# Third stage of a four-stage transformer block: who transposes P, and when the value product runs

## The reference

```
ln = layernorm(x)
q = ln @ Wq.T;  k, v = split(ctx @ Wkv.T)          # 16 heads of 32, 128 keys per sequence
s = where(causal, q @ k.T / sqrt(32), lowest)
p = softmax(s)
x = x + tanh(g) * (p @ v) @ Wout.T
```

## Time and profile before

| | |
|---|---|
| median of 3 runs | 1339.49 us (1338.63 to 1339.74) |
| profiled execution | 1338.95 us |
| its span, first to last instruction | 1337.2 us |
| granted TensorE clock | 1.000 |
| busy: TensorE, VectorE, ScalarE, GpSimd | 98%, 70%, 39%, 30% of the span |
| third stage | about 1004 to 1192 us of the span |

### The profile page before, as it was taken

How to read it: one execution, slowest core, us unless ns; L and a number is a source line. 1 busy time by engine, 2 the same in 40 slices (tenths; PEclk the granted TensorE clock), 3 DMA queues, 4 the chain that set the end, 5 groups by cost and what they waited for, 6 DMA issues and landing times.

```text
span 1337.2 us, 20281 instructions
## 1 busy us (share of the span) xinstructions
PE 1314.1 (98%) x7364; PEld 1065.7 (80%) x7364; DVE 937.2 (70%) x1813; ACT 517.5 (39%) x1569; POOL 404.5 (30%) x462
## 2 busy tenths in 40 slices
PE   7999999999999999999999999999998899999998
PEld 6788888888887788778887888788886677778877
DVE  5766676675775878785678667776888788846643
ACT  3545455454564331231123111321126777832220
POOL 3213423231255342201121112113525866630000
PEclk9999999999999999999999999999999999999999
DMA  8755454443572232210221112112324556455651
GB/s 297 229 165 167 151 171 137 157 158 120 190 217 87 88 90 72 83 40 16 57 78 52 31 40 87 44 48 67 99 83 145 198 177 206 163 200 172 218 167 55
DMA packets 137523, 167.92 MB, mean 126 GB/s; under 512 B 16080, under 2 KB 89936, under 8 KB 137424
## 3 DMA queue, kind: packets, MB, share of 16 engines
q1 hardware_dynamic: 137424, 166.63, 39.3%
HBM read 112.05 MB, written 54.53 MB: 125 GB/s over the span
## 4 chain that ended last, share of the span: by engine, by line
PE 88%; DVE 6%; ACT 3%; DMA 1%; issue 1%; POOL 1%; SPq 0%; ACTq 0%; DVEq 0%; POOLq 0%
PE bank L118 86%; PE bank L121 2%; ACT P L124 1%; DVE STG L130 1%; DVE AH L130 1%; DVE XR L140 0%; DVE AH L127 0%; ACT STG L124 0%; SPq L170 0%; DVE st L152 0%; DMA pscr<-STG 0%; DMA XR<-in_x_dram 0%; DMA STG<-in_W1E_dram 0%; DVE sm L146 0%; POOL AR L130 0%
## 5 line engine op out<-in xcount | busy, mean ns | idle before, releaser
L118 PE MATMUL bank<-XT,AR 128*128 128x512 f32 x1152 | 279.7, 392 | 0.1
L118 PE MATMUL bank<-AR 128*128 128x512 f32 x1056 | 257.7, 395 | 1.2 <-DVE AR L130 1.2
L118 PEld LDWEIGHTS bank<-XT,AR 128*128 128x128 f32 x1152 | 214.2, 188 | 47.0 <-ACT STG L124 0.5
L124 ACT ACTIVATE STG<-bank,b1c 128x512 f32<-128x512 f32 x128 | 88.3, 690 | 384.6 <-PE bank L118 318.0
L118 PEld LDWEIGHTS bank<-AR 128*128 128x128 f32 x1056 | 194.5, 188 | 49.1 <-issue 3.7
L118 PE MATMUL bank<-AR,CT 128*128 128x512 f32 x768 | 191.2, 392 | 0.0
L118 PE MATMUL bank<-AR,AH 128*128 128x512 f32 x768 | 185.5, 390 | 0.0
L127 DVE CAST AH<-STG 128x512 fp32r<-128x512 f32 x192 | 92.3, 481 | 110.7 <-PE bank L118 98.7
L118 PEld LDWEIGHTS bank<-AR,AH 128*128 128x128 f32 x768 | 143.9, 188 | 29.7
L118 PEld LDWEIGHTS bank<-AR,CT 128*128 128x128 f32 x768 | 140.2, 188 | 26.7
L127 POOL CAST BA<-STG 128x256 fp32r<-128x256 f32 x64 | 30.5, 477 | 394.5 <-PE bank L118 243.4
(11 more groups left out here) (145 smaller groups left out, 1814.3 us busy)
## 6 DMA issues: line engine op xcount, KB each, us to landing
XR<-scr SPq DMA_DIRECT2D x64, 256.0 KB, 3.1
pscr<-PYZ SPq DMA_DIRECT2D x30, 512.0 KB, 2.9
PYZ<-pscr SPq DMA_DIRECT2D x120, 128.0 KB, 3.0
XR<-in_x_dram SPq DMA_DIRECT2D x32, 256.0 KB, 4.2
XR<-lscr SPq DMA_DIRECT2D x128, 64.0 KB, 2.0
scr<-XR SPq DMA_DIRECT2D x32, 256.0 KB, 2.1
pscr<-STG SPq DMA_DIRECT2D x16, 512.0 KB, 2.6
PTV<-pscr SPq DMA_DIRECT2D x64, 128.0 KB, 2.8
```

The costliest lines, as they stand in the source:

```text
L118: return self.e.matmul(o, w, x, start=start, stop=stop, skip_group_check=True) if self.e else Nothing()
L124: return self.e.activation(o, x, func, **kw) if self.e else Nothing()
```

## The change

P of units 7 to 12 (`whole`) is transposed by VectorE in all four heads: two more block transposes into a new tile P3V, and a second store. DRAM holds both halves side by side (`pscr4`), and each of the four loads brings twice the data, into PTV[:, 0:2048]; the value product of these units reads all four heads in that layout (`P3W`). TensorE's transposes and ScalarE's copies go for these units. In steps 10 to 15 (`late_av`) the value product, and v of the next four sequences where it falls in the step, stand last in the step on TensorE, ScalarE and VectorE, and in steps 9 to 14 the loads stand behind SyncE's other loads. In all steps VectorE transposes P ahead of q's copy. The mask seeds are all ScalarE's (no seeded step has u % 4 = 2). In steps 2 and 3 two x transposes move from the one to the other, and one v product takes bank 4. Waits that named the bank of a transposed P name VectorE's transpose instead where that unit is whole. ScalarE's program has its calls moved as TensorE's.

```
+        P3V = sb("P3V", [128, 1024], F32)
...
+        P3W = PTV[:, 0:2048].rearrange("p (j n c) -> p n j c", j=4, n=16)
...
+        pscr4 = [nc.dram_tensor(f"pscr4{k}", [128, 2048], F32, kind="Internal").ap() for k in range(2)]
...
+        def whole(u):
+            return 7 <= u < 13
+
+        def late_av(u):
+            return 9 <= u < 18 and whole(u - 3)
...
         def by_vector(u):
-            return (0,) if u % 4 == 1 else (0, 1)
+            return () if u % 4 != 2 else (0, 1)
...
             def v3(m):
                 for b in range(4):
                     s = slice(128 * b, 128 * b + 128)
-                    k = ps.take(("v3", m, b), ring3.next())
+                    k = ps.take(("v3", m, b), 4 if (m, b) == (1, 0) else ring3.next())
...
             def turn3(u, ring):
-                for b in (2, 3):
+                for b in () if whole(u) else (2, 3):
...
-                        if j < 2:
+                        if whole(u):
+                            ins = pe.matmul(o.rearrange("p (a c) -> p a c", a=4), V3[:, b, 32 * h:32 * h + 32],
+                                            P3W[:, 4 * j + b], True, True)
+                        elif j < 2:
...
@@ the steps of TensorE @@
-                if 3 <= u < 16 and not k_first(u):
+                if 3 <= u < 16 and not k_first(u) and not late_av(u):
                     av3(u - 3, ring3)
-                if u > 4 and g == 2 and not k_first(u):
-                    v3(m)
+                    if g == 2:
+                        v3(m)
                 if 0 < u < 16:
                     k3(u, ring3)
...
+                if u == 3:
+                    ln_turn(2, 1, 0, ring3.next())
+                    ln_turn(2, 1, 1, ring3.next())
...
-                if u < 16 and g:
+                if u < 16 and g and u != 2:
                     for tb in tiles3(u)[g - 1]:
                         ln_turn(*after3(m), tb, ring3.next())
                 if u < 16 and g == 3 and m + 1 < NM:
                     cx_turn(m + 1, ring3)
                 if u < 16 and g == 3:
                     turn3(u - 2, ring3)
+                if late_av(u):
+                    av3(u - 3, ring3)
+                    if u < 16 and g == 2:
+                        v3(m)
...
@@ VectorE @@
+                for j in range(2) if whole(u) else ():
+                    e.wait_ge(*nm3_ok[u, 2 + j])
+                    if whole(u - 1):
+                        e.wait_ge(*t_p3v[u - 1])
+                    e.turn(blocks_out(P3V)[:, 4 * j:4 * j + 4],
+                           blocks_in(P3[:, u % 2, 1024:2048])[:, 4 * j:4 * j + 4]).then_inc(*p3y_ok.mark((u, 2 + j)))
...
                     for j in range(4):
                         largest(u - 1, j)
-                if 1 <= u < 16:
-                    q3_out(u)
+                if u >= 2:
+                    turn_p3(u - 2)
                 if u == 2:
                     ln_norm(2, 1, 0)
                     ln_norm(2, 1, 1)
-                if u >= 2:
-                    turn_p3(u - 2)
+                if 1 <= u < 16:
+                    q3_out(u)
...
@@ SyncE @@
-                e.dma(pscr[u % 2], P3Y).then_inc(*t_p3.mark(u))
+                if not whole(u):
+                    e.dma(pscr[u % 2], P3Y).then_inc(*t_p3.mark(u))
+                    return
+                to = pscr4[u % 2].rearrange("p (i h x) -> p h i x", i=4, h=2)
+                e.dma(to[:, 0], P3Y.rearrange("p (i x) -> p i x", i=4)).then_inc(*t_p3.mark(u))
+                e.wait_ge(*p3y_ok[u, 3])
+                e.dma(to[:, 1], P3V.rearrange("p (i x) -> p i x", i=4)).then_inc(*t_p3v.mark(u))
...
+                if whole(u):
+                    e.wait_ge(*t_p3v[u])
+                n = 2048 if whole(u) else 1024
+                src = (pscr4 if whole(u) else pscr)[u % 2].rearrange("(j r) (i x) -> i r j x", j=4, i=4)
                 for k in range(4):
-                    e.dma(PTV[32 * k:32 * k + 32, 0:1024].rearrange("r (j x) -> r j x", j=4), src[k]).then_inc(*d_p3.mark((u, k)))
+                    e.dma(PTV[32 * k:32 * k + 32, 0:n].rearrange("r (j x) -> r j x", j=4), src[k]).then_inc(*d_p3.mark((u, k)))
...
                 if u >= 2:
                     p3_store(u - 2)
-                    p3_load(u - 2)
+                    if not whole(u - 2):
+                        p3_load(u - 2)
...
+                if whole(u - 2):
+                    p3_load(u - 2)
                 for block in wo_at(u):
                     xf_store(*block)
```

More of the change, by code:

```diff
@@ L1077, in tensor @@
                     wo3(*block)
-                if u >= 16:
+                if u >= 16 and not late_av(u):
                     av3(u - 3, ring3)
@@ L1418, in exp3 @@
                     if u >= 2:
-                        ac.wait_ge(*(p3y_ok[u - 2, j] if j < 2 else ps.full(("pt3", u - 2, j))))
+                        ac.wait_ge(*(p3y_ok[u - 2, j] if j < 2 or whole(u - 2) else ps.full(("pt3", u - 2, j))))
                     for b in range(4):
@@ L1450, in h4 @@
                     else:
-                        ac.wait_ge(*ps.full(("pt3", 14, 3)))
+                        ac.wait_ge(*(p3y_ok[14, 3] if whole(14) else ps.full(("pt3", 14, 3))))
                         ac.wait_ge(*p3y_ok[14, 1])
@@ L1462, in scalar @@
                     exp3(u - 1, (0, 1))
-                if u >= 3 and not k_first(u):
+                if u >= 3 and not k_first(u) and not late_av(u):
                     av3(u - 3)
-                if values and not k_first(u):
+                if values and not k_first(u) and not late_av(u):
                     v3(m, 1)
@@ L1474, in scalar @@
                     av3(u - 3)
+                if u == 3:
+                    ln_turn(2, 1, 0)
+                    ln_turn(2, 1, 1)
                 if values and k_first(u):
@@ L1493, in scalar @@
                     turn3(u - 2, 3)
+                if late_av(u):
+                    av3(u - 3)
+                    if values and u < 16:
+                        v3(m, 1)
+                        v3(m, 3)
             av3(15)
@@ L2044, in vx4 @@
                 else:
-                    e.wait_ge(*(vy_ok[(t - 2) // 4, (t - 2) % 4] if t >= 2 else ps.full(("pt3", 15, 3))))
+                    e.wait_ge(*(vy_ok[(t - 2) // 4, (t - 2) % 4] if t >= 2 else (p3y_ok[15, 3] if whole(15) else ps.full(("pt3", 15, 3)))))
                 e.tt(VX[:, tb % 2, :].rearrange("p (k r) -> p k r", k=8), ps.ap(key)[:, :].rearrange("p (k r) -> p k r", k=8),
@@ L2051, in blocks4 @@
                 e.wait_ge(*ps.drained(("vx", m, tb)))
-                e.wait_ge(*(t_vy[tb % 2][t - 2] if t >= 2 else ps.full(("pt3", 15, 3))))
+                e.wait_ge(*(t_vy[tb % 2][t - 2] if t >= 2 else (p3y_ok[15, 3] if whole(15) else ps.full(("pt3", 15, 3)))))
                 e.turn(blocks_out(VY[:, tb % 2, :]), blocks_in(VX[:, tb % 2, :])).then_inc(*vy_ok.mark((m, tb)))
```

11 lines of the change are left out of this document (7 added, 4 removed).

## The result

| | before | after |
|---|---|---|
| median of 6 runs each | 1339.74 us | 1345.83 us (1344.34 to 1347.27) |
| ratio | | 1.0045 [1.0034, 1.0056] |
| profiled execution, span | 1338.95, 1337.2 us | 1345.45, 1343.5 us |
| granted TensorE clock over the span | 1.000 | 0.996 |
| DMA traffic | 167.92 MB | 174.21 MB |

The kernel became slower by 6 us. The forecast was 1340.7 us, no change that can be measured. The time lies above the range. Medians and ratios leave out two executions with a far lower granted clock: one of the kernel before (1457.74 us at 0.852) and one of E7 (1627.22 us at 0.754). Timelines, step lengths and waits come from one profiled execution of each kernel.

A forecast was written before the change was run, and what follows sets the result against it. TensorE, busy 98% of 1337.2 us, was taken as the bound. Early steps -0.4, step 9 +0.5, 10 +1.8, 11 to 13 -0.7, -1.4, -0.3, 14 +1.7 gave +1.2, so 1340.7 us; 8-in-10 range 1335.8 to 1344.5.

The forecast's parts named there:

- 2.5 us or more are to spare, and I cost them at nothing: Units 7 to 12: doubled loads of P, 4 to 7 us, would land before the value product a step later; cost nothing.
- rival C: Steps 11 to 15: P's loads become late and each step waits, five times; 1348 us at 10.5 us; chance 0.08.
- The granted clock should stay at full.: Sign to look for in the profile after: TensorE's granted clock not falling; no cost for it in the sum.
- Forecast A: Steps 10 and 14: waits for normalized x (XR) eat the six units' gain; 1338.8 to 1342.4 us; chance 0.50.
- Step 14's miss: Step 14 was forecast 1.7 us longer, TensorE waiting for XR with value and v products still to do.
- B: Steps 10 and 14: XR is not waited for, 2.8 and 2.5 us less; 1337.0, down to 1335.3 us; chance 0.20.
- Steps 11 and 12: Without P's transposes on TensorE, these steps were forecast 0.7 and 1.4 us shorter.
- The seeds' price: Mask seeds moved to ScalarE, between last exponential and next score pass: 0.51 us each; step 9 forecast +0.5 us.
- Step 13: Forecast 0.3 us shorter: value copy and P's copies go from ScalarE, one seed and an earlier subtraction come.
- Early steps: Steps 1 to 8: earlier P and moved x transposes shorten waits, but only 0.4 us is kept.
- E: Steps 2 to 6 give all that their waits hold, up to 3 us; 1337.6 us; chance 0.08.
- D: Six steps: four VectorE transposes ahead of q's copy delay normalizations and maxima by 0.7 us each; 1345 us; chance 0.14.

The follow-up runs named there:

- E7: Changed kernel with only units 8 to 10 whole, value product late only in steps 11 and 12, seeds and early x transposes as before; ratio 1.0014, 1341.36 us.
- E1: Changed kernel without the second store, the loads' wait for it and half of each load (old numbers read for two heads); ratio 1.0018, 1342.64 us.
- E9: Changed kernel with useless matmuls filling TensorE's waits ahead of x transposes in steps 10 and 14 and step 14's value product; ratio 1.0026.
- E8: Kernel before with only the four v products of steps 10 and 14 moved behind the x transposes; ratio 1.0025.
- E4: Changed kernel with mask seeds split as before, 12 by VectorE and 16 by ScalarE; ratio 1.0050.
- E12: Changed kernel with no unit whole and no late value product, its seeds, early x transposes, bank 4 and P order kept; ratio 1.0016.
- E6: Kernel before with only P's transposes by VectorE turned ahead of q's copy in all steps; ratio 0.9990, 1338.27 us.
- E3: Changed kernel with the two x transposes back in step 2 and the v product back in the rotation of banks; ratio 1.0035.
- E11: As E7, but with only unit 9 whole; ratio 1.0010.
- E5: E1 and E2 together on the changed kernel, part of the computation left out; ratio 0.9995, 1338.56 us.
- E2: Changed kernel with the late value and v products ahead of the next x's transposes on three engines; ratio 1.0051, 1347.47 us.

## Why the prediction was wrong

The failed step is this: "2.5 us or more are to spare, and I cost them at nothing". The spare time was counted from the end of the previous value product, with four loads of "4 to 7 us from first issue to last landing". Both terms were too small in step 13, whose loads step 14 needs. The loads did not start when the previous value product was done (1143.51) but 2.7 us later, when the second store of 5.94 us had landed; and they took 8.0 us. Together that is 10.7 us from the end of one value product, and the next one was wanted 8.6 us after it (1151.51 + 0.63 = 1152.14): it waited 2.17 us. The second store's landing stands nowhere in the sum, and the loads were priced by the median of a half-size load in a kernel where the DMA engines had room. The six units add 6.3 MB to steps whose engines were already busy 0.59 of the time; the share goes to 1.00, and transfers that the change doesn't touch get slower too (the last rows of E1). That is rival C's lateness in one step instead of five: 2.17 us in step 14. E1 shows the second stores and doubled loads together to be worth 3.6 us, part of which is the half clock behind their wait.

The second fault is a term that was not there at all: "The granted clock should stay at full." Forecast A itself put waits of 1 and 1.6 us into TensorE's queue, and gave them only their own length. In step 14 three waits (0.65, 1.43 and 2.17 us) are followed by 1.93 + 4.71 us for what takes 1.08 + 2.99 in step 10: 2.6 us more. Step 14's miss of 4.7 us is thus about 2.2 for the loads and 2.6 for the clock. E9 shows the second half by filling the waits (1.08 + 3.01 us for the same work, 2.5 us less over the kernel), and E1 that it comes without any wait for P (0.60 and 1.43 us, then 1.87 us for the value product), though 0.93 and 1.44 us did not bring it on in step 10 of the kernel after.

Point by point on the rest:
- XR's wait (A) was right in place and near in size: 0.93 + 1.44 us in step 10, 0.65 + 1.43 us in step 14, and step 10's +1.8 us to the tenth. B is out. E8, which moves only v and keeps P's transposes ahead, has a loss of the same kind. In step 14 XR was ready at 1147.22 + 4.14 = 1151.36, 0.5 us later than forecast, because the step began 0.3 us late instead of 0.5 us early.
- Steps 11 and 12 gained what was forecast, -0.6 and -1.6. The seeds' price of 0.5 us a step was right: step 9's +0.7 for +0.5, and E4 and E12 have it from both sides (the timeline puts that wait down to VectorE's ve, a statistic of the next x which the pass doesn't read; ScalarE's four seeds end beside it). The Trainium skill (Perfetto Trace Analysis, Optimizing Scalar/DVE Operations) says that offloading to ScalarE may make sense if VectorE is saturated. Here VectorE is busy 70%, so its condition isn't met, and the runs give no gain from the move: 3.5 us more in E12, nothing either way in E4, not 0.5 less.
- Step 13 gained nothing for -0.3. It isn't the wait of 0.70 us for P's loads: without it the step is as long (E1). It ends on ScalarE's seeds; with one seed fewer there it is 9.76 us (E4).
- Early steps, -0.2 for -0.4: the 2.04 us wait went and came back as bank waits in the step after (E6); the 1.65 us wait went for two of 1.01 us and a half clock of 1.4 us (E3). E is out; its bracket, 1.65 + 2.04 + 1.16 less 0.4, adds up to 4.45 us and not to 3.
- D did not come: in steps 9 to 15 the maxima begin 1.2 to 1.6 us after the pass does, but for step 12 with 2.3 us (before 1.4). What four block transposes ahead of q's copy did cost is a wait for q's bank (E7).

What stays open: how the loss at P's loads divides between the second store's landing and slower transfers; why a unit of whole P in step 11 delays an ordinary unit's value product in step 14 (E11); it wasn't followed. Nor is it shown what a gain from the 5.2 us of transposes would need: in E5 TensorE's timeline still has 1.69 and 1.11 us ahead of passes and the bank waits above. The best kernel here is E6, which takes neither the transposes nor the DMA, only the order of P and q.

## What to carry to other kernels

Price a doubled transfer with the DMA share of the very steps it falls in, not with the median of its half; where the share went to 1.00 here, stores and loads that nobody had changed became slower. Count the whole chain ahead of a load, every store it waits for included, and find which link ends last. When a forecast puts a wait into a dense TensorE stream, add the half clock behind it as a risk with its own price (1.3 to 2.6 us an event here, and not behind every wait). Before moving work behind a transpose, ask what that work was covering.

## What was not expected of the hardware

The granted clock falls to half after waits of TensorE that are short, and the same wait does not always bring it. It fell after 1.01 + 1.01 us (step 2 of the kernel after), 3.30 us (E2) and 0.65 + 1.43 + 2.17 us, and stayed full after 1.79 us ahead of step 10's pass in the kernel after and after 1.65 and 2.04 us in the kernel before. In step 10 it stayed full after 0.93 + 1.44 us in the kernel after and fell after 1.06 + 1.43 us in E3. In E5 it fell after 1.69 us: TensorE's timeline there has q's twelve matmuls at 4.61 us, against 3.02.

```profile
1098.53 1.17 PE L118 MATMUL bank<-MSK 32*128 32x128 f32 x32 [1.69 <-DVE ve L136]
1099.63 4.61 PE L118 MATMUL bank<-XT,AR 128*128 128x512 f32 x12
```

So it is a risk, with a price of 1.3 us (E2, step 10) to 2.6 us (step 14 of the kernel after) an event.

With the 16 DMA engines at a share of 1.00 the traffic was 288 GB/s over eleven microseconds of mixed loads and stores of 256 and 512 KB; in the shorter stretches above it was between 216 and 401 GB/s at shares of 1.03 to 1.08, so a full share does not stand for one rate. A load of 256 KB of P took 5.4 us in the median, up to 8.8; one of 128 KB in E12, 2.8. The Trainium skill, DMA: Bandwidth & Descriptors, Latency and other measured facts, has the access latency of the memory at 0.2 us on average and 2 us under high load. The trace agrees in direction; no run here separates latency from queueing.
